# Two attention heads in the two row halves of the matmul array, and a new order of a step's blocks

## The reference, cut to what matters

```python
# layer 0: 77 text tokens and 179 image tokens, each with its own softmax
q = split(x @ Wq.T); k = split(text @ Wk.T); v = split(text @ Wv.T)
out = attend(q, k, v) + attend(q, k_ip, v_ip)        # softmax(q k^T / 4) v, for each head
x = out @ Wo.T + bo + x
# layer 1: 252 text tokens, 4 image tokens, whose scores get a cosine of the mixed context
probs_t = softmax(q k_t^T / 4);  text_out = probs_t v_t
qsem = l2norm(probs_t @ text_ehs);  sem = qsem @ l2norm(ip_ehs)^T
probs_ip = softmax(q k_ip^T / 4 + 0.5 * sem) * spatial_mask
x = (text_out + probs_ip v_ip) @ W_out + b_out + x
```

## Time and profile before

| | |
|---|---|
| median of 3 runs | 808.07 us (805.87 to 808.98) |
| profiled execution: its own time | 806.63 us |
| its span, first to last instruction | 804.6 us |
| PE busy | 760.0 us, 94% of the span |
| PE's weight loads busy | 614.2 us, 76% |
| DVE busy | 570.8 us, 71% |
| ACT busy | 425.7 us, 53% |
| POOL busy | 403.9 us, 50% |
| granted clock of PE, mean | 0.994 of full |

### The profile page before, as it was taken

One profiled execution on the slowest core, in us unless ns is written; L12 is line 12 of the kernel. 1 busy time (PEld: TensorE's weight loads), 2 busy tenths in 40 slices (PEclk: granted clock), 3 DMA queues, 4 the chain that ended last, 5 costly groups with the idle time before them and its releaser, 6 DMA issues.

```text
span 804.6 us, 17019 instructions
## 1 busy us (share of the span) xinstructions
PE 760.0 (94%) x6246; PEld 614.2 (76%) x6246; DVE 570.8 (71%) x1579; ACT 425.7 (53%) x915; POOL 403.9 (50%) x299
## 2 busy tenths in 40 slices
PE   5889999999999999999999999999999999988796
PEld 5778688888888877877877788787777787766474
DVE  5357565757576666758768778698697797687765
ACT  5235546463646473646474565555655655545551
POOL 5512222020202040405568986797779778779873
PEclk9999999999999999999999999999999999999999
DMA  9854835664636472725353345144162332400010
GB/s 276 258 158 137 212 112 145 189 170 157 168 114 192 121 200 77 207 89 162 96 147 92 95 133 166 46 142 131 36 194 80 90 108 70 142 3 16 21 34 17
DMA packets 102514, 100.65 MB, mean 125 GB/s; under 512 B 9752, under 2 KB 101664, under 8 KB 102432
## 3 DMA queue, kind: packets, MB, share of 16 engines
q1 hardware_dynamic: 101952, 99.24, 42.4%
q10 hardware_dynamic: 480, 0.33, 0.2%
HBM read 61.65 MB, written 36.74 MB: 122 GB/s over the span
## 4 chain that ended last, share of the span: by engine, by line
PE 74%; DVE 8%; issue 5%; ACT 4%; POOL 4%; DMA 3%; SPq 2%; POOLq 0%; DVEq 0%; ACTq 0%
PE pB L388 20%; PE pB L519 12%; PE pB L482 8%; PE pB L505 7%; PE pB L603 5%; PE pPV L546 4%; PE pPV L541 4%; PE pPV L551 4%; PE pPV L537 3%; PE pB L560 2%; POOL Y L1352 2%; DVE m_sb L1101 2%; PE pB L415 2%; DMA KP<-k0d 1%; ACT P L876 1%
## 5 line engine op out<-in xcount | busy, mean ns | idle before, releaser
L1352 POOL TENSOR_TENSOR Y<-P,wv 128x512 f32<-128x512 f32 x120 | 157.1, 1325 | 104.4 <-ACT P L876 104.3
L1116 DVE TENSOR_TENSOR Y<-pB,Y 128x512 f32<-128x512 f32 x160 | 109.1, 686 | 64.2 <-PE pB L519 57.6
L482 PE MATMUL pB<-KP,QP 96*128 96x256 f32 x640 | 129.3, 287 | 4.0 <-DMA KP<-k0d 2.5
L1329 POOL TENSOR_TENSOR klo<-xin,khi 128x256 fp32r<-128x256 f32 x18 | 13.2, 755 | 230.9 <-ACT khi L787 230.9
L482 PEld LDWEIGHTS pB<-KP,QP 96*128 96x128 f32 x640 | 107.3, 192 | 16.4 <-issue 3.9
L1101 DVE TENSOR_REDUCE m_sb<-pB 128x2 f32<-128x504 f32 x160 | 108.0, 676 | 6.4 <-PE pB L482 5.2
L505 PE MATMUL pB<-QP,KP 100*128 100x512 f32 x320 | 108.8, 419 | 2.5 <-DMA QP<-mlo 1.8
L876 ACT ACTIVATE P<-pB 128x512 f32<-128x512 f32 x160 | 86.5, 596 | 39.0 <-PE pB L505 30.8
L866 ACT ACTIVATE wv<-pB 128x512 fp32r<-128x512 f32 x120 | 66.8, 591 | 67.8 <-PE pB L505 66.4
L876 ACT ACTIVATE P<-pB,ln 128x512 f32<-128x512 f32 x160 | 101.3, 692 | 0.0
L787 ACT ACTIVATE Vs<-pPV 128x512 f32<-128x512 f32 (+1 forms) x80 | 39.4, 492 | 102.9 <-PE pPV L541 70.1
(11 more groups left out here) (175 smaller groups left out, 1475.2 us busy)
## 6 DMA issues: line engine op xcount, KB each, us to landing
QP<-q0d SPq DMA_DIRECT2D x64, 192.0 KB, 3.9
KP<-k0d SPq DMA_DIRECT2D x64, 192.0 KB, 4.1
c_sb<-in_cT SPq DMA_DIRECT2D x16, 512.0 KB, 5.4
q0d<-qhi SPq DMA_DIRECT2D x32, 256.0 KB, 2.4
k0d<-khi SPq DMA_DIRECT2D x32, 256.0 KB, 2.4
q0d<-qlo SPq DMA_DIRECT2D x16, 256.0 KB, 2.5
k0d<-klo SPq DMA_DIRECT2D x16, 256.0 KB, 2.4
VB<-vipd SPq DMA_DIRECT2D x6, 640.0 KB, 3.9
```

The lines of the kernel that those rows point to most:

```text
L482: made = mm(bank[:, sc * S:sc * S + S], QP[i][0:KROWS, j, a, sc * 128:sc * 128 + 128], KP[i][0:KROWS, j, :], start=True, stop=True)
L1116: tt(Y[:, p, dst, :], bank_of["gp", q, dst][:, :], Y[:, p, dst, :], MUL).then_inc(dv_y, 1)
L1352: tt(Y[:, p, ch, :], P[:, p, ch, :], PH[q % HR][ch].bitcast(F32), SUB).then_inc(po_y, 1)
```

## The change

Each head of a pair now has its own half of the array's rows: head a lies in rows 64a to 64a+47 of QP and KP, with its maxima's rows in 64a+48 to 64a+51. `maxima` (new) works a pair at a time: four matmuls of 48 rows and 256 columns, in turn from the lower and the upper half, into two banks. `scores` has two forms. With `halves` it makes four matmuls of 52 rows and 256 columns, in turn from both halves, one bank for each head; without, it makes two of 116 rows and 512 columns as before. The form with halves is taken in the steps that also have maxima (0, 1, 2, 4, 5 and 6 of units 0 to 14, but for step 0 of units 0 and 1: 88 blocks).

Blocks move within a step: `weigh` stands ahead of scores and maxima where a step has halves, the maxima of up to two pairs follow the scores at once (before, the heads were spread over the step's pieces), then comes the first piece of the projections, and then the quads. ACT's exponentials of a step (`weights`) stand behind its copy of what was weighed. The maxima are spread over the steps as 2, 1, 2, 0, 2, 1, 2, 0, 0, 0 pairs (before: 3, 3, 3, 3, 3, 3, 2, 0, 0, 0 heads).

The rows of maxima go out by head, so each row takes two transfers. The indicator rows of KP are 16 for each half where they were 4. In units 8 and 9 the row of 1e20 comes by a transfer, and POOL's memset of QP goes. In layer 1 the packed loads of a step are issued on SP ahead of the step's results.

```diff
-KROWS = 96
-QROWS = 100
+KROWS = 48
+QROWS = 52
+IROWS = 16
...
-MAXH = (3, 3, 3, 3, 3, 3, 2, 0, 0, 0)
-MAXF = (3, 3, 3, 3, 2, 2, 2, 2, 0, 0)
+PAIRS = (2, 1, 2, 0, 2, 1, 2, 0, 0, 0)
+PAIRS_FIRST = (2, 1, 2, 1, 1, 1, 1, 1, 0, 0)
...
+    pairs = [("max", u + 1, jj) for jj in range(sum(many[:j]), sum(many[:j + 1]))] if u + 1 < U else []
+    late = u < 0 or (u, j) in LATE_MAX
+    halves = bool(pairs) and not late
...
-    if u >= B:
-        out += scores + weigh + [("quad", q, 0)] + first + [("quad", q, 1)]
...
+    if halves:
+        out += weigh + scores + pairs + weights + pieces[0] + quads + pieces[1]
     else:
-        out += scores + first + weigh
-    out += pieces[0] + pieces[1] + rest[:1] + pieces[2] + rest[1:]
+        out += scores + weigh + weights + quads + pieces[0] + pieces[1]
+    if late:
+        out += pairs
+    out += pieces[2]
...
-                for sc in range(2):
-                    made = mm(bank[:, sc * S:sc * S + S], QP[i][0:KROWS, j, a, sc * 128:sc * 128 + 128],
-                              KP[i][0:KROWS, j, :], start=True, stop=True)
...
+                banks = [take("mx", u * H + 2 * j + a) for a in range(2)]
...
+                for sc in range(2):
+                    for a, bank in enumerate(banks):
+                        rows = half(a, KROWS)
+                        made = mm(bank[:, sc * S:sc * S + S], QP[i][rows, j, a, sc * 128:sc * 128 + 128], KP[i][rows, j, :],
+                                  start=True, stop=True)
+                        if sc == 1:
+                            made.then_inc(pe_mx, 1)
...
+                banks = [take("sc", q, n) for n in range(2)]
                 for ch in range(2):
-                    bank = take("sc", q, ch)
-                    mm(bank[:, :], KP[i][0:QROWS, j, ch * 128:ch * 128 + 128],
-                       QP[i][0:QROWS, j, :, :].rearrange("p a s -> p (a s)"), start=True, stop=True).then_inc(pe_sc, 1)
+                    ts = slice(ch * 128, ch * 128 + 128)
+                    if halves:
+                        for a, bank in enumerate(banks):
+                            rows = half(a, QROWS)
+                            made = mm(bank[:, ch * S:ch * S + S], KP[i][rows, j, ts], QP[i][rows, j, a, :], start=True, stop=True)
...
+                        rows = slice(0, 64 + QROWS)
+                        mm(banks[ch][:, :], KP[i][rows, j, ts], QP[i][rows, j, :, :].rearrange("p a s -> p (a s)"),
+                           start=True, stop=True).then_inc(pe_sc, 1)
...
-                dma(QP[i][r:r + 1, :, :, :].bitcast(F32), tile[h0:h0 + H, :].bitcast(F32)).then_inc(l_m[i], 16)
+                for a in range(2):
+                    row = 64 * a + KROWS + r
+                    dma(QP[i][row:row + 1, :, a, :].bitcast(F32), tile[h0 + a:h0 + H:2, :].bitcast(F32)).then_inc(l_m[i], 16)
...
-                        nc.gpsimd.memset(QP[(u + 1) % 2][KROWS:QROWS, :, :, :].bitcast(F32), 1e20).then_inc(po_big, 1)
...
-                        elif what == "op" and u > B:
-                            result(*a)
...
+                    if u > B:
+                        for what, *a in plan(u, j):
+                            if what == "op":
+                                result(*a)
```

More of the change, by code:

```diff
@@ L99, in plan @@
         pieces = [[], [], []]
-    many = MAXF if u < 0 else MAXH
-    heads = [("max", u + 1, h) for h in range(sum(many[:j]), sum(many[:j + 1]))] if u + 1 < U else []
-    first, rest = heads[:1], heads[1:]
+    many = PAIRS_FIRST if u < 0 else PAIRS
+    pairs = [("max", u + 1, jj) for jj in range(sum(many[:j]), sum(many[:j + 1]))] if u + 1 < U else []
+    late = u < 0 or (u, j) in LATE_MAX
+    halves = bool(pairs) and not late
     out = []
@@ L105, in plan @@
         out += [("shift", u + 1)]
-    scores = [("scores", q + 1)] if u >= 0 and q + 1 < U * NP else []
+    scores = [("scores", q + 1, halves)] if u >= 0 and q + 1 < U * NP else []
     weigh = [("weigh", *divmod(q // 2 - 1, NG))] if q >= 2 and q % 2 == 0 else []
-    weigh += [("weights", q + 1)] if scores else []
-    if u >= B:
-        out += scores + weigh + [("quad", q, 0)] + first + [("quad", q, 1)]
-    elif (u, j) in LATE_MAX:
-        out += scores + weigh
-        rest = heads
-    else:
-        out += scores + first + weigh
-    out += pieces[0] + pieces[1] + rest[:1] + pieces[2] + rest[1:]
+    quads = [("quad", q, 0), ("quad", q, 1)] if u >= B else []
+    weights = [("weights", q + 1, halves)] if scores else []
+    if halves:
+        out += weigh + scores + pairs + weights + pieces[0] + quads + pieces[1]
+    else:
+        out += scores + weigh + weights + quads + pieces[0] + pieces[1]
+    if late:
+        out += pairs
+    out += pieces[2]
     if q >= 2 and q % 2 == 0:
@@ L495, in shift_rows, with scores @@
                 give(bank)
-            def scores(q):
+            def scores(q, halves):
                 u, j = divmod(q, NP)
@@ L518, in quad @@
                 for n, (col, src) in enumerate(jobs):
-                    made = mm(bank[:, :], G[i][:, col:col + 128], ph[src], start=(n == 0), stop=(n == len(jobs) - 1))
+                    made = mm(bank[:, :], G[i][:, col:col + 128], ph[:, src, :, :].rearrange("p a s -> p (a s)"), start=(n == 0), stop=(n == len(jobs) - 1))
                 made.then_inc(pe_gp, 1)
@@ L708, in tensor_program @@
                 if u < 0:
-                    scores(0)
+                    scores(0, False)
             weigh(U - 1, NG - 1)
@@ L857, in shift_rows, with split, scored, rounded_weights @@
                     rows_out(ac, nc.scalar.dma_start, u, ROWS_HI)
-            def rounded_weights(q):
+            def split(tile, n, halves):
+                return tile[:, :, n, :] if halves else tile[:, n, :, :]
+            def scored(q, n):
+                return bank_of["sc", q, n][:, :].rearrange("p (x s) -> p x s", s=S)
+            def rounded_weights(q, halves):
                 k = q - B * NP
-                for ch in range(2):
-                    ac.wait_ge(pe_sc, 2 * q + ch + 1)
+                for n in range(2):
+                    ac.wait_ge(pe_sc, 2 * q + n + 1)
                     ac.wait_ge(pe_gp, 2 * (k - HR) + 2)
@@ L865, in rounded_weights, with weights @@
                     ac.wait_ge(pe_bg, job_no(B - 1, "V2"))
-                    act(PH[q % HR][ch], bank_of["sc", q, ch][:, :], ACT.Exp, scale=0.25).then_inc(ac_ph, 1)
-            def weights(q):
+                    act(split(PH[q % HR], n, halves), scored(q, n), ACT.Exp, scale=0.25).then_inc(ac_ph, 1)
+            def weights(q, halves):
                 twice = {"bias": ln2[:, 0:1]} if q >= B * NP else {}
-                for ch in range(2):
-                    ac.wait_ge(pe_sc, 2 * q + ch + 1)
+                for n in range(2):
+                    ac.wait_ge(pe_sc, 2 * q + n + 1)
                     ac.wait_ge(pe_pv, (q - PR) // 2 + 1)
```

126 lines of the change are left out of this document (68 added, 58 removed).

## The result

The changed kernel takes 814.95 us (median of 6 runs, 812.78 to 820.16), the one before 807.66 (805.87 to 810.21) beside it: a ratio of 1.0102, with a 95% interval of 1.0076 to 1.0128. It is slower by 1.0%, where I had forecast 804.2. The profiled execution took 815.98 us, 9.4 more than that of before.

A forecast was written before the change was run, and what follows sets the result against it. PE, busy 94% of the span, was taken as the bound. Terms -38.1 - 20.1 + 16.2 + 28.8 + 1.8 + 4.8 + 4.8 - 2.0 = -3.8 took 806.6 to 802.8 us, median 804.2; range 783 to 826, the forecast's own 796 to 812.

The forecast's parts named there:

- Maxima -38.1: 160 pairs of heads: maxima run two by two in row halves, 0.238 us a pair for 0.476, saving 38.1 us.
- scores -20.1: 88 score blocks become two groups of 0.119 us instead of two matmuls of 0.233, saving 20.1 us.
- The rival of serial weight loads: Every group of two: weight loads of the halves stay serial, groups 0.22 apart; +22.9, 831 us, chance 0.12.
- Changes of the array's shape +16.2: 138 added changes of array shape around halves, at 0.117 us each, cost 16.2 us (0 to 27.2).
- my rival at 0.13: Each change of shape costs the full 0.197 us: changes 27.2, sum +3.2, 811 us; chance 0.13.
- The bank wait +28.8: Layer 1, units 8 to 13: quads wait for score banks until ACT writes P, 4.8 us a unit, 28.8 us.
- Given back -2.0: Layer 1's shorter load queue, POOL's memset and the second quad's wait for DVE give back about 2.0 us.
- The maxima's transpose +4.8: Layer 0, four heads at step 6's start: transpose waits 0.6 us for DVE in eight units, 4.8 us (0 to 10).
- Row transfers and loads +4.8: Layer 0: four mhi and four mlo issues delay key loads, some 0.6 us a unit, 4.8 us (0 to 20).
- POOL's memset: Counted among the items that together give back about 2.0 us; no size of its own.
- 1.8 (unit 14, not measured apart): Unit 14 has no projections, so one bank more; only the second quads wait, 1.8 us.

The follow-up runs named there:

- e11: Changed kernel with layer 0's scores on the full array again, ahead of the weighing, number of shape changes kept: 828.04 us, ratio 1.0230.
- e6: e1 plus 13 to 24 dummy identity transposes at each of six places where PE waits: 801.10 us, ratio 0.9933 to the kernel before.
- e10: e9 plus dummy identity transposes in six waits: 789.38 us, ratio 0.9790 to the kernel before.
- e1: Changed kernel with layer 1's pairs of maxima ahead of the scores in steps with halves, so quads take other banks: 802.88 us, ratio 0.9952.
- e4: Changed kernel with one of step 6's two pairs of maxima moved to step 3: 811.73 us, ratio 1.0056.
- e9: e5 with the quads behind the second third of the projections' pieces in steps 0, 2, 4 of layer 1: 787.53 us, ratio 0.9759.
- e12: Changed kernel with only the quads behind the second third of the projections' pieces in steps 0, 2, 4 of layer 1: 810.87 us, ratio 1.0049.
- e5: Changed kernel with the edits of e1 and e4 together: 799.13 us, ratio 0.9900 to the kernel before.
- e7: Changed kernel with one full-array transpose before every block of scores in halves in layer 0: 826.11 us, ratio 1.0255.

## Why the prediction was wrong

The sign was wrong: -3.8 us forecast for the profiled execution, +9.4 measured. The time lay within the range, but above the 796 to 812 of the forecast itself. By the forecast's own steps:

*Maxima -38.1, scores -20.1: right.* The groups follow at 0.12, and e11 gives back the scores' share where it should. The rival of serial weight loads is out.

*Changes of the array's shape +16.2: this step failed.* I read 0.117 into 32 columns and 0.197 out of them in the earlier trace rows and took the lower one, arguing that halves use several tiles as the weighing does. But the 0.117 was the excess over the weighing's own pace of 0.216, in which each group already carries a weight load that isn't covered. A group of halves follows at 0.12, so it has nothing to set against the change and pays the whole 0.2, in and out. 138 x 0.196 is 27.0: +10.8 to the sum. A steady unit of layer 0 tells the two prices apart: 37.5 - 2.38 (maxima) - 1.37 (scores) + 8 x 0.196 + 0.74 + 0.2 (the waits below) = 36.3, for 36.2 measured; at 0.117 it would be 35.6. The full price was my rival at 0.13. Its sum of +3.2 was still too low, since it let the bank waits shrink and they did not. The Trainium skill (TensorEngine Tiling, Tiling Modes, Key Properties) says that changing the mode drains the engine, and the trace agrees at all these places. The two rows had different paces beneath them; the price was to be taken from the one whose pace the new work has.

*The bank wait +28.8: right in place and mechanism, 4.8 too small.* For unit 11 the trace names P for 2.7 + 0.8 us, and 0.3 in step 5, where the first quad waits for DVE's ST, a bank and a releaser that I had not in the forecast: 3.8 in all at six places. With up to 0.29 that each loses beyond its idle time that is 5.6 us a unit for 4.8, 33.6 if all six units were like this one. By the distances of the ends half of the difference sits in step 2 (1.44 for 1.0), where ACT came late, and half in step 5 (0.59 for 0.2). *Given back -2.0: too small.* Before, the second quad and the transpose idled for 0.6 and 0.3 in a unit of layer 1, 1.3 us by the distances of the ends, which the new waits cover: -7.9. On top, the weighing waits for Y: 0.10 idle and 0.3 by the distances, +1.8. These three together are 0.7 off, but only because the first two were mis-sized by 4.8 and 5.9 in opposite directions, which is luck.

*The maxima's transpose +4.8: right in place, a little too large.* In six units of layer 0 it now idles for 0.59 where it did not, put to DVE:

```profile
231.52 0.38 PE L504 MATMUL pB<-ident,m_sb 128*40 128x128 f32 x2 [0.59 <-DVE m_sb L1127]
...
237.46 0.63 PE L582 MATMUL pB<-ident,Vs 128*128 128x128 f32 x4 [0.21 <-ACT Vs L809]
```

From the end of the work ahead (230.34 + 0.60) to the end of the first transpose (231.90 less its pace of 0.11) it is 0.85, so 0.74 are lost in each, 4.4 us. In the first and the last of the eight it waited before as well, for 2.02 and 0.98, now for 1.73 and 0.64. That leaves +3.8.

*Row transfers and loads +4.8: too large.* The four issues do hold ACT for 3.05 us and SP for 3.15:

```profile
232.34 3.05 ACTq L802 DMA_DIRECT2D QP<-mhi  x4
...
232.84 3.15 SPq L802 DMA_DIRECT2D QP<-mlo  x4
```

But in the steady units the rows were there when PE wanted them. What is left is ACT's delay: the transpose of the weighed values in step 8 waits some 0.2 us in six units, 1.3.

*POOL's memset, in the -2.0 given back: of the wrong sign.* The row of 1e20 for layer 1 now comes by a transfer (QP<-ind), behind the rows on SP, and PE waits for it once:

```profile
350.15 1.47 SPq L1487 DMA_DIRECT2D QP<-ind  x2
...
352.99 0.74 PE L526 MATMUL pB<-QP,KP 116*128 116x512 f32 x2 [1.73 <-DMA QP<-ind]
```

The kernel before has no wait there.

*Not in the forecast: the clock.* The profiled execution had a mean granted clock of 0.983, that before 0.994. Two stretches of equal length in the changed kernel, columns as above:

```profile
284.40:287.80 3.40, 3.40 (x18) 3.35 (x16) 3.27 (x11) 1.41 (x3) 1.08 (x2) 0.50 0.26 89
300.00:303.40 3.40, 3.40 (x29) 3.13 (x29) 2.96 (x10) 1.08 (x2) 0.00 (x0) 1.00 0.26 70
```

At the lower of the two levels, 1.2 GHz, PE did 18 matmuls for 29 (of not quite the same kinds). This stretch stands behind 2.38 us in which PE waited for ACT:

```profile
282.63 0.66 PE L582 MATMUL pB<-ident,Vs 128*128 128x128 f32 x4 [2.38 <-ACT P L904]
...
284.45 1.22 PE L394 MATMUL pB<-khi,wq 128*128 128x256 f32 x4
```

The four matmuls of 256 columns take 1.22 us, for 0.64 at the full clock. At most the clock costs the share that is missing, 0.017 x 814.2 - 0.006 x 804.6 = 9.0 us, less where PE would have waited anyway. What one such stretch costs can be read once, at the same place of units 12 and 13, with the same waits ahead of it:

```profile
626.38 1.88 PE L541 MATMUL pB<-wkv 128*128 128x512 f32 x7 [0.16 <-ACT P L904]
628.10 1.05 PE L394 MATMUL pB<-wvi,cc 128*128 128x324 f32 x6
...
683.43 3.09 PE L541 MATMUL pB<-wkv 128*128 128x512 f32 x7 [0.16 <-ACT P L904]
686.32 1.44 PE L394 MATMUL pB<-wvi,cc 128*128 128x324 f32 x6
```

From the first quad to the transpose of the maxima it is 2.83 us in unit 12 and 4.39 in unit 13, where the mean granted clock is 0.61, and unit 13 takes 58.6 us where units 11 and 12 take 57.1. So this stretch cost 1.5 us. What brought the clock down there is not shown: unit 12 had the same waits and kept it.

The balance of the profiled execution: -38.1 - 20.1 + 27.0 + 33.6 + 1.8 (unit 14, not measured apart) - 7.9 + 1.8 + 3.8 + 1.3 = +3.2. Measured is +9.4. The 6.2 that are left are not only the clock. The balance takes every unit of layer 1 like unit 11 and leaves out what happens once, and the trace has waits of that kind that the kernel before does not have: 2.38 us at 282.63 (above), 1.73 for the row of 1e20, and in step 2 of unit 9 2.66 where the steady units have 1.17:

```profile
430.82 3.07 PE L541 MATMUL pB<-wkv 128*128 128x512 f32 x7 [2.66 <-ACT P L904]
```

Others went: the first maxima wait 1.0 us less for keys, and in unit 14 a wait of 2.19 for P is gone where the quads now wait 1.71. How much of the 1.0% is the clock's and how much these single waits' stays open. Filling the waits (e6, e10) raised the clock without gaining time, but with costs of its own. With the rest of the forecast kept as it was, the price of the shape changes turns its -3.8 into +7.0, or into the rival's +3.2 if the waits shrink as I had them shrink.

## What to carry to other kernels

Price a change of the array's shape by the pace of the work that stands around it, count the changes in the new order, and group what shares a shape. When work on the bound engine gets shorter or is bunched, list which bank each next block takes and who frees it: here the whole gain of layer 1 hung on that, and three moves of blocks in the table (e1, e4, e9) turned 1.0% slower into 2.4% faster. Where a bank comes late because another engine waits in order, take another bank first: coming later gained 4.1 us on the late bank (e12) and 11.6 once the bank was another (e9 behind e5). When a fill of dummy work is put in a wait, look in the trace whether it stands in the wait or behind it.

## What the runs showed of the hardware

- Two matmuls of 48 or 52 rows in the two row halves run wholly at once: 0.12 us for a pair of 256 columns, the pace of a single one before.
- Going between the full array, row halves and 32-column tiles costs 0.2 us each way at the places read: the next group ends 0.30 to 0.33 us behind the last, where its stream takes 0.12. Between 128 and 64 columns it costs nothing. A transpose behind such a change ended 0.26 us after the weighing (e7).
- The granted clock differs between executions of one program, and the time with it: the twelve runs of e4 go from 805.60 us at 0.991 to 816.53 at 0.975, and those of the kernel before from 803.21 at 0.998 to 813.58 at 0.984. That is some 7 us for 0.01 between the ends, and it goes with most of the scatter between runs; which of the two brings the other such a list can't tell. One stretch at the lower level cost 1.5 us in unit 13, with all else alike. A difference of 0.5% needs many runs here.
